# Cross-attention and expert layers: half of the probability turns moved from TensorE to VectorE and DMA

## The reference

```python
x = x + xattn(layernorm(x), ctx)      # 16 batches of 256 rows, 256 wide; context 192 wide; 16 heads of 64
x = x + ffn(layernorm(x))             # 8 experts, top 2, capacity 640, hidden 1024

def xattn(x, context):
    q, k, v = heads(x @ w_q), heads(context @ w_k), heads(context @ w_v)
    attn = softmax(einsum('bhid,bhjd->bhij', q, k) * 64 ** -0.5)
    return einsum('bhij,bhjd->bhid', attn, v) @ w_o + b_o
```

## Time and profile before

| | |
|---|---|
| runs | 988.52, 988.68, 991.03 us; median 988.68 |
| the profiled execution | 991.04 us; span of its instructions 989.1 us |
| attention, periods 6 to 61 | about 94 to 703 us of the span |
| TensorE, VectorE, ScalarE busy | 97%, 79%, 63% of the span |
| mean granted TensorE clock | 0.997 of 2.4 GHz |
| data moved by DMA | 56.75 MB |

### The profile page before, as it was taken

How to read it: one execution, slowest core, us unless ns; L and a number is a source line. 1 busy time by engine, 2 the same in 40 slices (tenths; PEclk the granted TensorE clock), 3 DMA queues, 4 the chain that set the end, 5 groups by cost and what they waited for, 6 DMA issues and landing times.

```text
span 989.1 us, 23198 instructions
## 1 busy us (share of the span) xinstructions
PE 956.1 (97%) x8364; PEld 865.1 (87%) x8364; DVE 782.8 (79%) x2081; ACT 622.9 (63%) x1712; POOL 282.6 (29%) x440
## 2 busy tenths in 40 slices
PE   7889999999999999999999999999889999999995
PEld 7778888888888888888888888888778999999995
DVE  6897778888888888888888888877886777787762
ACT  5777776777767776777777777777734433344420
POOL 5541121313142222313132241302433333221233
PEclk9999999999999999999999999999999999999998
DMA  8550101011010101011010101000243856455422
GB/s 222 158 131 2 33 2 33 23 34 55 2 54 13 35 14 34 13 32 45 2 44 6 33 9 33 16 2 16 87 135 78 167 117 136 93 88 129 112 27 27
DMA packets 85792, 56.75 MB, mean 57 GB/s; under 512 B 47164, under 2 KB 81578, under 8 KB 85552
## 3 DMA queue, kind: packets, MB, share of 16 engines
q1 hardware_dynamic: 76848, 46.30, 17.6%
q0 software_dynamic: 8832, 8.98, 5.3%
HBM read 36.01 MB, written 24.20 MB: 61 GB/s over the span
## 4 chain that ended last, share of the span: by engine, by line
PE 80%; DVE 11%; ACT 3%; issue 3%; POOL 1%; DMA 0%; another core or an unknown queue 0%; POOLq 0%; DVEq 0%; ACTq 0%
PE psum L626 23%; PE psum L723 11%; PE psum L709 10%; PE psum L693 9%; PE psum L865 9%; PE psum L881 9%; PE psum L740 8%; DVE prob L1138 2%; DVE hidl L1075 2%; DVE bufl L1075 1%; ACT prob L942 1%; DVE hidh L1351 1%; ACT hid L1047 1%; PE psum L638 1%; DVE negmax L1127 1%
## 5 line engine op out<-in xcount | busy, mean ns | idle before, releaser
L942 ACT ACTIVATE prob<-psum,negmax 128x256 f32<-128x256 f32 x512 | 240.0, 487 | 89.1 <-DVE negmax L1127 89.1
L892 ACT ACTIVATE probt<-psum 128x512 f32<-128x512 f32 x256 | 157.3, 623 | 45.8 <-PE psum L709 44.8
L1127 DVE TENSOR_REDUCE negmax<-psum 128x2 f32<-128x512 f32 x256 | 160.1, 682 | 24.4 <-PE psum L693 22.7
L1138 DVE TENSOR_SCALAR prob<-prob,invtot 128x256 f32<-128x256 f32 x512 | 166.7, 389 | 4.5
L709 PE MATMUL psum<-ident,prob 128*128 128x128 f32 x1024 | 150.7, 273 | 2.7 <-DVE prob L1138 1.6
L1047 ACT ACTIVATE hid<-psum,b1t 128x640 f32<-128x640 f32 x64 | 50.8, 796 | 129.5 <-PE psum L865 129.5
L709 PEld LDWEIGHTS psum<-ident,prob 128*128 128x128 f32 x1024 | 119.7, 140 | 12.3 <-ACT probt L892 2.2
L723 PE MATMUL psum<-probt,v 128*64 128x256 f32 x1024 | 124.6, 385 | 0.0
L563 POOL DMA_INDIRECT slot_table<-row,picki x64 | 64.9, 1013 | 173.8 <-DVE picki L1299 147.9
L602 POOL DMA_INDIRECT out_rows<-y,rowi x40 | 66.3, 1658 | 161.7 <-DVE y L1361 154.8
L942 ACT ACTIVATION_READ_ACCUMULATOR prob<-psum,negmax 128x1 f32 x512 | 112.1, 219 | 0.0
(11 more groups left out here) (196 smaller groups left out, 2652.7 us busy)
## 6 DMA issues: line engine op xcount, KB each, us to landing
w1r<-in_w SPq DMA_DIRECT2D x8, 1024.0 KB, 5.4
w2r<-in_w SPq DMA_DIRECT2D x8, 1024.0 KB
slot_table<-blank SPq DMA_DIRECT2D x8, 662.5 KB, 9.4
blocks<-slot_table SPq DMA_DIRECT2D x56, 80.0 KB
xin<-in_x SPq DMA_DIRECT2D x16, 256.0 KB, 2.9
out_rows<-x SPq DMA_DIRECT2D x16, 256.0 KB, 3.2
c<-in_ctxt SPq DMA_DIRECT2D x16, 128.0 KB, 3.1
c<-in_ctxt SPq DMA_DIRECT2D x32, 64.0 KB, 2.9
```

What stands on the lines that cost most here:

```text
L892: copy = lambda dst, src, **kw: act.activation(dst, src, ACT.Copy, **kw)
L942: last = act.activation(prob[:, m % 2, u, qb, :], psum[:, u, qb * S:(qb + 1) * S], ACT.Exp, bias=negmax[:, m % 2, u, qb:qb + 1], accum_out ...
L1127: dve.tensor_reduce(negmax[:, m % 2, u, :], psum[:, u, :].rearrange("p (q s) -> p q s", q=ST), AX.X, ALU.max, negate=True).then_inc(sem("m ...
L1138: last = dve.tensor_scalar(prob[:, m % 2, u, qb, :], prob[:, m % 2, u, qb, :], invtot[:, m % 2, u, qb:qb + 1], None, ALU.mult)
```

## The change

In periods 6 to 61 (`MOVED`) only units 2 and 3 are turned by TensorE. Units 0 and 1 go another way: ScalarE's exp writes their probabilities regrouped in pieces of 32 columns; VectorE turns every 32x32 square in place (**square0**, **square1**, `dve.transpose`); SyncE writes the 512 KB to memory (**lift**) and reads them back with the squares' places exchanged (**move**, four DMAs of 128 KB, runs of 1 KB) straight into `probt`. pv reads its moving side for that pair in pieces of 32 columns.

In all periods the scaling moves behind pv: VectorE takes the eight reciprocals of a period and turns them (**inv**), SyncE writes them to memory (**inv_out**, 128 runs of 128 bytes) and reads them back spread over 64 partitions per head (**inv_in**, two DMAs), and VectorE multiplies the output of pv in PSUM (**a_norm**, 128x512) before ScalarE takes its high part. turn waits for exp instead of norm.

logits of the first 13 batches leave the three banks for bank 4, which turn 3 uses; turn 3 waits for bias in those periods. pv and logits come directly behind scores, xt, o, x2t and pos at the end of the period; the orders of ScalarE, VectorE, GpSimd and SyncE are listed anew. scatter moves from a batch's fourth period to the first period of the batch after, in which TensorE makes an o product, and waits for q. `xn` and `x2t` share one buffer, so x2t_sb waits for xt and ln1 for logits. The clearing of the slot table is spread over periods 2 to 4. After the change, the once-per-batch DMAs are called **traffic**.

```diff
+MOVED = range(6, PERIODS - 2)
+def by_pe(m):
+    return (2, 3) if m in MOVED else (0, 1, 2, 3)
...
     for m in range(1, PERIODS - 2):
         b, r = divmod(m, PER_B)
+        four = len(by_pe(m - 1)) == 4
+        out += [("scores", m)] + ([("pv", m - 2)] if m >= 2 else [])
+        out += [("logits", b - 2)] if r == 3 and 2 <= b else []
+        if four:
+            out += [("q", m + 1), ("turn0", m - 1), ("k", m + 1), ("turn1", m - 1), ("v", m), ("turn2", m - 1)]
         else:
+            out += [("q", m + 1), ("turn2", m - 1), ("k", m + 1), ("turn3", m - 1), ("v", m)]
         if r == (1 if b else 2) and b + 1 < B:
+            out += [("xt", b + 1)]
+        if r == 2 and 1 <= b:
+            out += [("o", ST * (b - 1))]
         if r == 2 and 2 <= b:
+            out += [("x2t", b - 2)]
         if r == 0 and 2 <= b:
             out += [("o", ST * (b - 2) + 1)]
+        out += [("turn3", m - 1)] if four else []
+        out += [("pos", b - 3)] if r == 1 and 3 <= b else []
+        out += steps("exp0 exp1", m) + ([("a_hi", m - 2)] if m >= 2 else []) + [("q_hi", m + 1)]
...
+            out += [("copy2", m - 1), ("k_hi", m + 1), ("exp2", m), ("copy3", m - 1), ("exp3", m), ("v_sb", m)]
+        if r == (1 if b else 2) and b + 1 < B:
+            out += [("xt_hi", b + 1)]
+        out += [("copy3", m - 1)] if four else []
+        out += [("gate_exp", b - 3)] if r == 0 and 3 <= b else []
+        out += [("x2t_sb", b - 2)] if r == 2 and 2 <= b else []
+        out += steps("max0 max1", m) + ([("x2add", ST * (b - 2) + 1)] if r == 1 and 2 <= b else [])
+        out += ([("split_lo", 5)] if m == 1 else []) + steps("max2 max3", m)
+        out += ([("a_norm", m - 2)] if m >= 2 else []) + [("inv", m - 1)]
+        out += [("slot", b - 3)] if r == 2 and 3 <= b else []
+        out += [("bias", b - 2)] if r == 3 and 2 <= b else []
+        out += [("ln1_stats", 1)] if m == 1 else []
+        out += ([("a_lo", m - 2)] if m >= 2 else []) + [("q_lo", m + 1)]
+        out += [("square0", m)] if m in MOVED else []
+        out += [("k_lo", m + 1)]
+        out += [("square1", m)] if m in MOVED else []
+        if r == 0:
+            out += steps("shift compare rank gate", b - 3) if 3 <= b else []
+            out += [("ln1", b + 1)] if 1 <= b < B - 1 else []
+        if r == 1:
+            out += [("ln2_stats", b - 2)] if 2 <= b else []
+            out += [("xt_lo", b + 1)] if 1 <= b < B - 1 else []
+        if r == 2:
+            out += steps("ln1 xt_lo", 1) if b == 0 else []
+            out += [("ln2", b - 2)] if 2 <= b else []
+            out += [("ln1_stats", b + 2)] if b + 2 < B else []
+            out += [("keys", b - 3)] if 3 <= b else []
+            out += [("x2add", ST * (b - 1))] if 1 <= b else []
+        out += [("pick", b - 3)] if r == 3 and 3 <= b else []
...
+        out += [("scatter", b - 4)] if r == 0 and 4 <= b else []
+        out += [("residual", b + 1)] if r == 0 and 1 <= b < B - 1 else []
+        out += [("ln2_root", b - 2)] if r == 1 and 2 <= b else []
...
+        out += steps("inv_out inv_in", m - 1) + (steps("lift move", m) if m in MOVED else [])
+        out += {2: steps("clear", 0), 3: steps("clear", 1), 4: steps("clear", 2)}.get(m, [])
+        out += [("traffic", b - 2)] if r == 1 and 2 <= b else []
...
-APART = {("x2t", B - 2): 2, ("logits", B - 2): 3, ("pos", B - 2): 4, ("logits", B - 1): 4}
+APART = {**{("logits", b): 4 for b in range(B - 3)}, ("x2t", B - 2): 2, ("logits", B - 2): 3, ("pos", B - 2): 4, ("logits", B - 1): 4}
...
+            def inv_out(m):
+                sp.wait_ge(sem("inv"), m + 1)
+                sp.dma_start(inv_table[m % 2].rearrange("j (a i) -> a j i", a=GROUPS), invturned[:, m % 2, :])\
+                  .then_inc(sem("inv_out"), 16)
+            def inv_in(m):
+                sp.wait_ge(sem("inv_out"), 16 * (m + 1))
+                if m >= 1:
+                    sp.wait_ge(sem("a_norm"), m)
+                for h in range(2):
+                    sp.dma_start(invrows[h * HD:(h + 1) * HD, :, :],
+                                 inv_table[m % 2][0:UNITS * ST].rearrange("(c h q) p -> h c (q p)", h=2, q=ST)[h]
+                                 .partition_broadcast(HD))\
+                      .then_inc(sem("inv_in"), 16)
+            def lift(m):
+                sp.wait_ge(sem("square"), 2 * (m - MOVED[0] + 1))
+                if m - 2 in MOVED:
+                    sp.wait_ge(sem("pv"), m - 1)
+                sp.dma_start(square_table[m % 2], prob_pair(m)).then_inc(sem("lifted"), 16)
+            def move(m):
+                sp.wait_ge(sem("lifted"), 16 * (m - MOVED[0] + 1))
+                sp.wait_ge(sem("pv"), m - 1)
+                for g in range(GROUPS):
+                    sp.dma_start(probt_pair(m)[g * SQ:(g + 1) * SQ, :].rearrange("j (a c) -> j a c", a=GROUPS),
+                                 square_table[m % 2].rearrange("(a j) (g c) -> g j a c", a=GROUPS, g=GROUPS)[g])\
+                      .then_inc(sem(f"moved{m % 2}"), 16)
...
                 if u == 3:
-                    pe.wait_ge(sem("probt"), UNITS * m + 1)
-                pe.wait_ge(sem("norm"), UNITS * m + u + 1)
+                    pe.wait_ge(sem("probt"), turns_to(m, 0))
+                    if m % PER_B == 2 and 2 <= m // PER_B < B - 1:
+                        pe.wait_ge(sem("biased"), m // PER_B - 1)
+                pe.wait_ge(sem("exp"), UNITS * m + u + 1)
...
+                if m in MOVED:
+                    pe.wait_ge(sem(f"moved{m % 2}"), 16 * moves_to(m))
...
+                            if m in MOVED and cc == 0:
+                                p = probt_pair(m).rearrange("p (a u k q i) -> p u k q a i", a=GROUPS, u=2, k=ST, q=ST)[:, h, kb]
...
+                if m >= 2 and u in by_pe(m - 2):
+                    act.wait_ge(sem("turn"), turns_to(m - 2, u))
+                elif m >= 2:
+                    act.wait_ge(sem(f"moved{m % 2}"), 16 * moves_to(m - 2))
...
+            def a_norm(m):
+                dve.wait_ge(sem("pv"), m + 1)
+                dve.wait_ge(sem("inv_in"), 32 * (m + 1))
+                at = work_bank("pv", m).rearrange("p (c s) -> p c s", c=2)
+                dve.tensor_tensor(at, at, invrows[:, :, :], ALU.mult).then_inc(sem("a_norm"), 1)
+            def square(m, u):
+                dve.wait_ge(sem("exp"), UNITS * m + u + 1)
+                at = prob_pair(m).rearrange("p (g u c) -> p u g c", g=GROUPS, u=2)[:, u]
+                dve.transpose(at, at).then_inc(sem("square"), 1)
```

More of the change, by code:

```diff
@@ L76, in timeline @@
             *steps("max2 max3", 0), ("split_hi", 4), *steps(k, 1), ("exp1", 0), ("split_lo", 4),
-            *steps("exp2 exp3 v v_sb", 0), ("split_hi", 5), *steps(half[0], 0)]
+            *steps("exp2 exp3 v v_sb", 0), ("split_hi", 5)]
     for m in range(1, PERIODS - 2):
         b, r = divmod(m, PER_B)
[L80 to L94, removed]
-        else:
-            out += steps(half[1], m - 1) + (steps("ln1_stats ln1_root", 1) if m == 1 else []) + steps(q, m + 1)
@@ L97, in timeline @@
[L97 to L105, removed]
@@ new lines, in timeline @@
+        out += [("pos", b - 3)] if r == 1 and 3 <= b else []
+        out += steps("exp0 exp1", m) + ([("a_hi", m - 2)] if m >= 2 else []) + [("q_hi", m + 1)]
+        if four:
+            out += [("copy0", m - 1), ("exp2", m), ("k_hi", m + 1), ("copy1", m - 1), ("exp3", m), ("copy2", m - 1),
+                    ("v_sb", m)]
+        else:
+            out += [("copy2", m - 1), ("k_hi", m + 1), ("exp2", m), ("copy3", m - 1), ("exp3", m), ("v_sb", m)]
+        if r == (1 if b else 2) and b + 1 < B:
+            out += [("xt_hi", b + 1)]
@@ new lines, in timeline @@
+        if r == 2:
[5 more added lines that the diff above has]
+        out += [("pick", b - 3)] if r == 3 and 3 <= b else []
+        out += {1: [("ln1_root", 1)]}.get(m, [])
+        out += [("ctx", b + 1)] if r == 0 and b + 1 < B else []
+        out += {1: [("vsplit", 1)], 2: [("constants", 0)], 3: [("residual", 0), ("residual", 1)], 4: [("vsplit", 2)],
+                5: [("vsplit", 3)]}.get(m, [])
@@ L137, in timeline @@
             ("logits_part", o1), ("spread", 0), ("spread", 1), ("pos", e), ("base", 0), ("spread", 2), ("spread", 3)]
-    out += [*steps("exp0 exp1", m), ("a_hi", m - 2), ("q_hi", z), ("copy0", m - 1), ("exp2", m), ("k_hi", z),
-            ("x2t_sb", c), ("copy1", m - 1), ("exp3", m), ("copy2", m - 1), ("v_sb", m), ("w_hi", 0), ("w_hi", 1),
-            ("copy3", m - 1), *steps("exp0 exp1", z), ("a_hi", m - 1), ("copy0", m), ("exp2", z), ("copy1", m),
+    out += [*steps("exp0 exp1", m), ("q_hi", z), ("a_hi", m - 2), ("copy2", m - 1), ("k_hi", z), ("exp2", m),
+            ("copy3", m - 1), ("exp3", m), ("v_sb", m), ("x2t_sb", c), ("w_hi", 0), ("w_hi", 1),
+            *steps("exp0 exp1", z), ("a_hi", m - 1), ("copy0", m), ("exp2", z), ("copy1", m),
             ("exp3", z), *steps("copy2 copy3", m), ("gate_exp", c), ("v_sb", z), ("w_hi", 2), *steps("copy0 copy1", z),
```

(1 more changed line is left out.)

186 lines of the change are left out of this document (102 added, 84 removed).

## The result

The changed kernel takes **958.35 us** (median of 4 runs, 957.82 to 959.79) against 988.86 us (988.52 to 991.03) for the kernel before: a ratio of 0.9689, 95% interval 0.9672 to 0.9707.

What follows compares the result with a forecast made beforehand. TensorE's work was taken to bound each period. 44.8 us of removed turns, less 18.2 of stalls, plus 1.6 at the start gave 28.2; 991.0 became 962.8, less the 2.4 above the median: 960.5 us, range 940 to 986.

Steps and rivals of the forecast that it cites:

- the offset: Whole kernel: the profiled execution stood 2.4 us above the median of 988.7, so 962.8 became 960.5 us.
- The removed turns: TensorE, 14 batches: two of four turns leave each period, 3.2 us a batch, 44.8 us in all.
- r0 to r3: A batch's four periods, m mod 4 = 0 to 3, with TensorE work of 12.11, 9.87, 12.60 and 9.66 us.
- the change of product shape: TensorE, turn ahead of scores: 0.17 of its 0.53 us may stay for v or o ahead of scores.
- The stall in r3: TensorE's next scores wait for exp3, behind k_hi and copies on ScalarE: 0.55 us a batch.
- K: Moment when TensorE goes from k to the turn behind it; exp3 ends K + 3.1, wanted at K + 2.6.
- The stall in r2: TensorE's k waits for slot, behind a_norm and the inverses on VectorE: 0.75 us a batch.
- The batch: Main loop: a middle batch of 42 to 43 us, where it was 44.24.
- The start: Early in the kernel: TensorE's one wait of 1.63 us for a scaling goes, a gain of 1.6 us.
- The tail: Last periods: the inverses' new round trip stands against the scalings that go; taken as 0, within 4 us.
- The split read: pv's 32-column moving side: taken as 0, at most 55 us; as a rival 1015 us, chance 0.05.
- SyncE's loop: SyncE's DMA chain: 9.5 us a period, between 8.2 and 12.0; as the bound, a rival of 1014 us, chance 0.08.

Runs made afterwards that it cites:

- both: Changed kernel with slot ahead of a_norm and the inverses on VectorE, and exp2 between a_hi and q_hi on ScalarE: 952.28 us, ratio 0.9626.
- both_traffic_w: The kernel both, with once-a-batch DMAs issued between inv_out and inv_in, and w_hi 0 and 1 behind the last v copy: 935.06 us, ratio 0.9467.
- w_later: Changed kernel with ScalarE's two copies of the first expert weights (w_hi 0 and 1) moved behind the last v copy: 953.58 us, ratio 0.965.
- no_move: Changed kernel without lift and move; pv reads old values for units 0 and 1, exp0 and exp1 wait for the squares: 954.21 us, ratio 0.9637.
- lift_twice: Changed kernel with each lift's 512 KB written a second time, to memory nobody reads, and move waiting for both: 1024.87 us in one run.

## Why the prediction was right

The sum held because its mechanism did. That it came within 2.2 us is in part luck: terms that were off partly cancelled, and the offset (last point) halved what was left.

- **The removed turns: right, undersized.** 3.2 us a batch were forecast. Without stalls a batch takes 40.56 us (`both`, both_traffic_w) against 44.24: 3.68. By period r0 to r3 it is 0.89, 0.98, 0.94 and 0.87, for 0.72, 0.88, 0.80 and 0.80. The term that was mis-sized is the change of product shape: v ahead of scores pays 0.10 where I let 0.17 stay, and the rest of the change around turns went with them.
- **The stall in r3: right place, undersized.** 0.55 was forecast, 0.75 came. From K (424.08) the exponential ends 3.1 us later, as chained. TensorE wants it earlier than K + 2.6, by the smaller shape change, and pays about 0.1 to start again.
- **The stall in r2: right, in two pieces.** slot begins 5.84 us into r2 and k 6.11; the forecast was 6.1 for k. Of the 0.75 that were forecast (the terms themselves, 6.12 less 5.41, give 0.71) 0.51 came there. Another 0.22 came in r2's scores, where I had written that xt and pos cover r1's exponentials (0.74): they take 0.64, and the cover fell short. 1.48 a batch, not 1.3.
- **The batch:** 44.24 - 3.68 + 1.48 = 42.04, forecast 42.3. Over 14 batches the gain is 30.8 where I had 26.6; between the starts of periods 6 and 62 it is 31.4, as the first whole batch, without slot, gains more.
- **The start: right sign, undersized.** Period 6 begins at 69.50 us instead of 72.72 (the 94 us in the table of the kernel before are the start of period 8). Between the starts of periods 0 and 6 TensorE is idle for 4.4 us instead of 7.5. The 1.63 us wait went; another part, which I had not counted, is the wait of xt for its rows in period 2, 1.64 us before and 0.38 after. 3.2 instead of 1.6.
- **The tail: within its bounds, by another mechanism.** The gain at period 62 is 34.6, in the span 33.0, so 1.6 is lost behind it. I had the round trip of the inverses against the scalings that go. What lost time is a weight load that stands behind the loop in SyncE's order and holds ScalarE, and the lower clock behind TensorE's wait for it, of which the prediction had nothing; w_later gives 4 to 5 us back (by the ratios 3.9, by the medians 4.8). I had listed who waits for SyncE's queue in the loop, but not what stands behind the loop in it.
- **The split read, the square, a_norm:** from pv to q it is 1.88 us with and without pieces; the price of nothing was right and the bound of 55 us fell. By the Trainium skill (SBUF — State Buffer, Door 1: The DMA port swizzle) consecutive accesses to one 16-byte line run at full bandwidth, which 32 adjacent floats meet; this run agrees, with that 1.88 us. The square takes 702 ns for 670, a_norm 695 for 690.
- **SyncE's loop: undersized, without harm to this kernel.** It is the weakest step of the prediction. 9.5 us a period were forecast. In `both`, where it is the bound, its steps average, over some fifty loops, 2.61 us from inverses out to in (2.1 taken), 1.49 from there to the lift (1.1), 3.88 from lift to move (3.4) and 1.88 from move to out (2.3): 9.9 for 8.9, and with 0.67 of old traffic 10.5. Each step was priced by one transfer on a quiet queue; here each has a spread (lift to move 3.35 to 5.52, out to in 1.98 to 6.83), and the chain adds the means. The page of the kernel before could have warned: there 256 KB take 2.9 (x in) and 3.2 us (x out) in the median, where several transfers go out together. I gave that rival 0.08 for a loop 1 us below the period. The margin in the changed kernel was 0.35 us a period (0.8 in w_later, the same program up to period 62), and a_norm waited for inverses four times, 2.5 us in all, where I had 2 to 4 us to spare. The loop did not bind here, as no_move shows, but lift_twice shows what lay behind that margin.
- **The offset.** The sum was made against the profiled 991.0, 2.2 to 2.4 above the median, and I took all of it off. The profiled run after is 0.5 below its own median. The sum for the profiled run was 962.8 and 957.8 came; a good part of the closeness in the median is the offset.

## What to carry to other kernels

When a queue runs a chain of dependent round trips once a period, its length is a bound like an engine's busy time, though no busy share shows it: add up issue to issue from the trace, and compare with the shortest period that the other edits can reach, not with today's. Whatever has to go through the same queue belongs into a gap where the chain waits anyway; on the variant `both` that was worth 13 us. And when work is taken off the bounding engine, follow each queue it now uses to the last instruction of the kernel: what stands behind the loop in program order is late too. Price a wait of TensorE together with the granted clock behind it: in the tail here a wait of 2.7 us cost more than 5, while the stalls of 0.3 to 0.5 us in the batches left the clock at 1.00.

## What was not expected of the hardware

- The size of a transfer told little of its round trip: from the issue of the 16 KB of inverses to SyncE's next step it took 2.40 us in the median and 2.56 on average, more than the 2.1 us to landing of a lone 256 KB; 32 times as much (512 KB) took 3.64 and 3.75. In no_move, where no move goes out just ahead of them, the same inverses took 1.97 and 2.05.
- Half-loaded DMA engines cost TensorE nothing: with 153 and with 53 GB/s moving, a batch took 42.05 and 42.02 us.
